# A graph network kernel on one core: sorting scatters issued in runs of five, each run answered by SP before the next

## What is computed

```python
edge_index = jnp.stack([src, dst])
h = jnp.maximum(_layernorm(x, axis=-1), 0.0)
x = x + _L0_gnn_ref(h, src, dst, ...)
h = jnp.maximum(_layernorm(x, axis=-1), 0.0)
x = x + _L1_gnn_ref(h, edge_index, ...)
h = jnp.maximum(_layernorm(x, axis=-1), 0.0)
x = x + _L2_gnn_ref(h, edge_attr_64, ..., edge_index, 3125)
h = jnp.maximum(_layernorm(x, axis=-1), 0.0)
x = x + _L3_gnn_ref(h, ..., src, dst)
```

## Time and profile before

| | us |
|---|---|
| median of 3 runs | 3888.61 |
| lowest and highest run | 3878.62, 3900.84 |
| the profiled execution, its own time | 3879.7 |
| span of its trace, first to last instruction | 3878.0 |
| share of the span: PE, DVE, ACT, POOL | 48%, 57%, 29%, 41% |
| granted TensorE clock, mean over the span | 0.663 of full speed |

### The profile page before, as it was taken

The page is one execution under the profiler, slowest core; times in us unless marked ns, Lnnn a source line. Parts: engine busy times, 40 slices in busy tenths (PEclk is TensorE's granted clock), DMA queues, the critical chain, the costliest instruction groups (busy, mean ns, idle before and its releaser), DMA issues. The chain is left out here.

```text
span 3878.0 us, 58297 instructions
## 1 busy us (share of the span) xinstructions
PE 1844.2 (48%) x16222; PEld 1335.8 (34%) x16222; DVE 2228.1 (57%) x4872; ACT 1128.6 (29%) x3658; POOL 1594.2 (41%) x1665
## 2 busy tenths in 40 slices
PE   6745555555545555411412147762111465665387
PEld 5623333333333333310101135751101355554222
DVE  7777777777777777411301013341111599997899
ACT  1154554445445454300001002100000011115644
POOL 1055555555555555376766640027676200000000
PEclk9865555555555555655655569975555689986599
DMA  7812221212112222622222210024443222220000
GB/s 250 307 41 43 46 43 43 43 43 46 42 43 43 43 44 47 246 65 51 60 54 53 51 34 1 12 82 125 121 115 76 74 87 78 88 78 31 0 0 9
DMA packets 399308, 267.12 MB, mean 69 GB/s; under 512 B 321456, under 2 KB 349293, under 8 KB 399073
## 3 DMA queue, kind: packets, MB, share of 16 engines
q1 hardware_dynamic: 306278, 87.81, 10.6%
q10 hardware_dynamic: 41472, 118.96, 8.4%
q0 software_dynamic: 51488, 59.40, 6.1%
HBM read 158.59 MB, written 107.47 MB: 69 GB/s over the span
## 5 line engine op out<-in xcount | busy, mean ns | idle before, releaser
L1241 POOL DMA_INDIRECT sorted_edges<-r_load,r_to x800 | 794.1, 993 | 675.0 <-DMA r_to<-places 364.6
L807 POOL DMA_INDIRECT hsrc<-h,edges x808 | 778.1, 963 | 593.1 <-PE ps L1004 361.4
L1004 PE MATMUL ps<-AO,hsrc 125*64 125x64 f32 x1616 | 195.9, 316 | 310.3 <-remote 252.7
L1555 ACT ACTIVATE w_work<-w_work 128x384 f32<-128x384 f32 (+1 forms) x160 | 85.8, 536 | 839.7 <-DVE w_work L1756 723.8
L1049 PE MATMUL ps<-hot,lo 125*128 125x400 bf16 (+2 forms) x1000 | 273.6, 456 | 100.9 <-DVE hot L866 70.8
L875 DVE TENSOR_TENSOR prod<-ps,hsrc 125x1024 f32<-125x1024 f32 x200 | 244.1, 1221 | 110.3 <-issue 107.8
L1004 PEld LDWEIGHTS ps<-AO,hsrc 125*64 125x64 f32 x1616 | 179.9, 224 | 346.0 <-issue 346.0
L1031 PE MATMUL ps<-rwin,there 120*125 120x256 bf16 x800 | 178.7, 397 | 242.4 <-DVE there L850 218.3
L866 DVE TENSOR_SCALAR hot<-ramp,small 125x400 bf16<-125x400 int16 x800 | 210.8, 321 | 143.5 <-issue 139.6
L1756 DVE TENSOR_TENSOR w_work<-ps,w_work 128x384 f32<-128x384 f32 (+1 forms) x160 | 90.9, 568 | 312.6 <-remote 264.9
L1409 PE MATMUL ps<-R 128*128 128x64 bf16 x3000 | 140.8, 208 | 247.0 <-DVE R L1745 121.9
(11 more groups left out here) (412 smaller groups left out, 3945.1 us busy)
## 6 DMA issues: line engine op xcount, KB each, us to landing
w_work<-sorted_edges ACTq DMA_DIRECT2D x42, 1000.0 KB
r_load<-in_edge_attr_dram SPq DMA_DIRECT2D x80, 312.5 KB
dstrow<-dst_rows SPq DMA_DIRECT2D x101, 234.4 KB
sorted_edges<-A ACTq DMA_DIRECT2D x10, 2000.0 KB, 9.8
A<-counts SPq DMA_DIRECT2D x12, 1600.0 KB
counts<-A ACTq DMA_DIRECT2D x4, 4000.0 KB, 31.7
sorted_edges<-A ACTq DMA_DIRECT2D x15, 1000.0 KB, 9.5
hsrc<-h,edges POOLq DMA_INDIRECT x808
```

What stands on the lines that cost most here:

```text
L807: g.indirect_dma_start(out=hsrc[:, s, t, :], out_offset=None, in_=S.h0[:, :], in_offset=bass.IndirectOffsetOnAxis(ap=edges.bitcast(I32)[:, ...
L1004: mm = pe.matmul(sums.rearrange("d (h w) -> d h w", h=H)[:, :, OFF[t]:OFF[t] + SUB], hsrc[0:TP, s, t, :], AO[0:TP, t, :, :], start=(t == 0 ...
L1241: g.indirect_dma_start(out=S.sorted, out_offset=bass.IndirectOffsetOnAxis(ap=to[:, hf, t:t + 1], axis=0), in_=load[:, hf, t, :], in_offset ...
```

## The change

HALF stays 10, RUN is 5, so that a chunk has RUNS = 4 runs. After each five scatters POOL adds one to `run` and waits for `go`. SP waits for `run`, adds three to `step` one by one (nobody waits for `step`), and then one to `go`. In `both(c)` the two answers of a half come before the wait for its landing. The semaphores that only carry waits are now one (`qr["carrier"]`).

```diff
+    STRIDE = 3
+    RUN = HALF // 2
+    RUNS = 2 * HALF // RUN
...
+            def follow(c, hf):
+
+                for r in range(RUNS // 2):
+                    sp.wait_ge(qr["run"], c * RUNS + hf * (RUNS // 2) + r + 1)
+                    for _ in range(STRIDE):
+                        sp.sem_inc(qr["step"], 1)
+                    sp.sem_inc(qr["go"], 1)
+
             def both(c):
 
                 for hf in range(2):
+                    follow(c, hf)
                     sp.wait_ge(qr[f"sc{hf}"], c * (16 * HALF) + 16 * HALF)
                     sp.sem_inc(qr["ready"], 1)
                     bring_half(nc, I, S, sp, c + 1, hf)
...
             for hf in range(2):
+                follow(C2 - 1, hf)
                 sp.wait_ge(qr[f"sc{hf}"], C2 * 16 * HALF)
...
                     for t in range(HALF):
                         g.indirect_dma_start(out=S.sorted, out_offset=bass.IndirectOffsetOnAxis(ap=to[:, hf, t:t + 1], axis=0),
                                              in_=load[:, hf, t, :], in_offset=None).then_inc(qr[f"sc{hf}"], 16)
+                        if t % RUN == RUN - 1:
+                            g.sem_inc(qr["run"], 1)
+                            g.wait_ge(qr["go"], c * RUNS + hf * (RUNS // 2) + t // RUN + 1)
+                            g.sem_inc(qr["carrier"], 1)
```

More of the change, by code:

```diff
@@ L1145, in spread @@
     props = [{n: sem(f"c_{n}{k}") for n in ("prod", "free", "own", "sum") if (n, k) != ("sum", 1)} for k in range(4)]
-    cl = {n: sem("k_" + n) for n in ("tp", "xt", "y", "t", "y1", "yfree", "hi", "r", "mid", "lo", "out", "wd", "carrier")}
-    qr = {n: sem("r_" + n) for n in ("sc0", "sc1", "ready", "carrier", "acarrier")}
+    cl = {n: sem("k_" + n) for n in ("tp", "xt", "y", "t", "y1", "yfree", "hi", "r", "mid", "lo", "out", "wd")}
+    qr = {n: sem("r_" + n) for n in ("sc0", "sc1", "ready", "carrier", "run", "step", "go")}
     qm = {n: sem("m_" + n) for n in (
@@ L1326, in turn_block @@
                 pe.wait_ge(cl["xt"], b + NB)
-                pe.sem_inc(cl["carrier"], 1)
+                pe.sem_inc(qr["carrier"], 1)
                 pe.transpose(S.bank[5][0:D, 0:P], fresh[:, m, :], S.ident[:, :]).then_inc(cl["tp"], 1)
@@ L1564, in _ @@
                 act.wait_ge(qm[f"es{s}"], n * 16 + 16)
-            act.sem_inc(qr["acarrier"], 1)
+            act.sem_inc(qr["carrier"], 1)
         @block.vector
```

## The result

| | before | changed |
|---|---|---|
| median, same chip (us) | 3883.61, 4 runs | 3526.94, 4 runs |
| lowest and highest | 3877.05, 3900.84 | 3497.86, 3531.55 |
| the profiled execution | 3879.7 | 3531.55 |
| its span | 3878.0 | 3529.8 |

The ratio is 0.907 (95% interval 0.904 to 0.910): 357 us less, where 190 were forecast. The time lies inside the range and on the side that was given 0.67. It lies 172 us under the forecast (3699) and 116 above the rival in which SP's signals carry PE's along (3411).

What follows compares the result with a forecast made beforehand. Signals held while scatters fly were taken to bound 1640 to 3046 us. With 9.3 us runs and the chain at 0.55, the last item ends at 3320 instead of 3510, giving 3690, plus 9 for the median: 3699 us, range 3440 to 3980.

Steps and rivals of the forecast that it cites:

- the rival in which SP's signals carry PE's along: Beside scatters, SP's increments let PE's held signals through: chain at 0.7, run 7.7 us, total 3411 us; chance 0.15.
- What bounded the kernel: From 1640 to 3046 us, scatters in flight hold PE's signals and slow SP's steps; POOL's pauses let them go.
- A run takes 9.3 us: In the sort, five scatters take 6.4 us plus a 2.9 us draining pause; between 6.75 and 13.1 us.
- SP's loads "just covered": SP's loads, 6.2 us a half, are as long as POOL's five scatters, so they should not delay answers.
- I take 0.55 for both stretches: Beside scatters, convolution and items go at 0.55 of free speed, with 0.4 and 0.8 as ends.
- The sum: After 1640 us: convolution done 2488, items from 2523, scatters until 3111, last item 3320 instead of 3510; gain 190 us.
- its likeliest case alone: Forecast for the whole kernel without rivals: 3560 to 3840 us, chance 0.46, nearly all of it faster.
- The moved scatters: 15 of chunk 23's scatters wait behind the convolution, costing POOL 19 us, which the compute chain gets as undisturbed time.
- The slower one: SP's answer is held like PE's signals: pause 6.1 us, run 12.5, total 3994 us, tipping at run 11.8; chance 0.24.
- The rival of prompt answers: Answers to POOL come in 0.35 us, scatters stay in flight, the chain creeps as before: 3883 us; chance 0.12.
- VectorE barring GpSimd: DVE work slows late scatters, five taking 9.3 us longer in 67 runs: about 4138 us in all; chance 0.03.
- The signs that were named: In the changed profile: gaps 2 to 4 us behind each five, last scatter near 3110, convolution wait under 60 us.

Runs made afterwards that it cites:

- its nearest relative: Changed kernel with SP answering each run with one increment instead of four; on chips without held signals, ratios 1.081, 1.076 and 1.078 against the kernel before.

## Why the prediction was right, and where its sizes were off

**What bounded the kernel: right for this chip.** Held signals were read from a few stalls and from the busy shares. The changed kernel shows signals arriving in the pauses, and the two kernels that differ by POOL's wait alone, 3564 and 3863 us, show that its waiting is what pays. What is held was read too narrowly: not only PE's signals but the steps of PE and SP themselves, 0.70 us and multiples of it. And "pauses of POOL let them go" left out that the pauses of the kernel before, 60 us of them until 2290, did it late or not at all. The chips on which no signal is held show the same from the other side: DVE works beside the scatters there without any pause. That a chip of the second kind exists could not be seen in the one trace of before.

**"A run takes 9.3 us": the step that failed.** It rested on "I take 2.9", a pause behind every five in which the scatters drain. Measured: nothing behind the second five of a half, and 3.3 on the mean behind the first. The answer does not wait for a drain at all, nor even for the writing: POOL's signal goes 4.4 or 8.0 us before the fifth scatter is written. POOL reached the wait for the convolution at 2330.6 instead of 2468, so the 90 runs from 1637.0 took 694 us, 7.7 each. The other 67, from 2361.0 to 2939.6, took 8.6.

**SP's loads "just covered": wrong, and the reason for the pause.** The sum of 6.2 us was about right (6.06 at 1913.67). It left out when the loads begin: 1.7 us after the half's last scatter is written. So they end 1.4 us after POOL's next five, and POOL's next scatter starts another 1.2 us later. Had I laid the start of the loads beside POOL's five, this would have stood in the sum. SP starts them soon now: 1.7 us after the half's last scatter, where the median of the kernel before is 5.4.

**"I take 0.55 for both stretches": too low.** By the prediction's own working, 475 us of work are due until the convolution ends. The last 29 ran in POOL's wait, so 446 fell in the 691 us before: 0.65. For the items 23 of 13.3 us in 540 us give 0.57, though POOL paused less than assumed. The term that was too small is the free time after a pause: 2 us of it from `attend`, with 1.4 of the pause itself, 3.4 in a run of 9.3, while the trace has some 7 us in each half of 15.2. With the prediction's own 0.3 for the rest that gives, as an estimate, 0.46 + 0.54 x 0.3 = 0.62.

**The sum.** With 7.7 and 8.6 us for a run and 0.65 and 0.57 for the chain: POOL's wait at 2331, the convolution done at 2360, items from about 2400 (forecast 2523), last scatter 2939 (3111), 160 - 93 = 67 adds or 17 items of 13.3 left, end at 3163 (3320; the last add L1773 starts at 3158). The 157 us between the forecast and this are nearly the whole error: 3699 - 3527 = 172. Both sizes were wrong in the same direction, and the gain is nearly twice the one forecast. The time lies outside what the prediction gave its likeliest case alone (3560 to 3840); that it lies in the range is owed to the width left for the rival at 3411, whose reason was not the right one.

**The moved scatters** cost and gave what was said: POOL waited 30.5 us before 2361, and the chain's last 29 us ran undisturbed.

**The rivals.** The slower one, an answer that is held as PE's signals are, did not come. Pauses of six microseconds are not the rule: the mean is 3.3, and a mean run of 7.7 or 8.6 us is far from the tip of 11.8. Behind 2361, of the eight pauses over 5 us five follow loads of 8.4 to 10.8 us, which the chips without held signals show too, and the others loads that begin 3.8 to 5.0 us after the half instead of 1.7. The rival of prompt answers was half right. After the second five of a half the answer is prompt, so prompt that POOL does not stop; if it had been so after each, the nearest run is the kernel without the wait, which gained 31 us. The rival of SP's signals that carry PE's along fits the times best (7.7 us a run, POOL's wait at 2325, 0.7), but for another reason: its runs are short because every second answer is free. Its own effect, read without POOL's wait, is those 31 us at most; whether the increments do more together with a pause was not run where signals are held. VectorE barring GpSimd: a scatter beside the items takes 333.71 / 315 = 1.06 us, against 1.004, and 1.09 in the kernel without the wait on a chip without held signals (366.27 / 336, stretch 2000 to 2473), where DVE is busy 350 of 473 us. By the Trainium skill's rule (SBUF — State Buffer, SBUF: two separate sides), that descriptors and VectorE's two-port modes exclude each other, the trace agrees in sign; it is some 0.06 us a scatter, 18 us in all, where 1.86 a scatter was priced for the rival.

**The signs that were named.** Convolution wait under 60 us: 23. More than 20 items before the last scatter: 23. PE's share over 35%: 59%. Right. Last scatter near 3110 and gaps behind each five: wrong, as above. The sign that was named for SP's increments, gaps under 1 us with DVE busy, is met by every second gap; the kernel without the wait decides that it did not mean them.

**What stays open.** Whether a pause without SP brings the same where signals are held (the kernels for it met only chips without); whether four increments are better than one there, or pauses after every five; whether it matters that POOL is silent while SP issues the last of its loads, as it is in these pauses; what in the chip slows the steps of PE and SP and lets a held signal go, and why one kind of chip holds them and the other does not. No version beat the rest on both kinds: the changed kernel is the best of the three run where signals are held, and the kernel before, or the one without POOL's wait, the best of those run on the three other chips.

## What to carry to other kernels

When every engine is idle beside a stream of indirect DMAs, look how late each signal arrives after its producer's end. Look also how far apart an engine's instructions are that wait for nothing. If it is microseconds, a short, regular stop of the issuing engine can pay: about 240 us of pauses bought 299 us here, since the engine had to wait for the others later anyway. Where such a stop is made of a handshake, look when the signal is really given, since the queue can run ahead of the work, and what the answering engine is doing at that moment, since that sets the length of the stop, far more than the number of increments does. And run both kernels on more than one chip before keeping such a change: it is 9% faster on one kind, while its nearest relative is 8% slower on the other.

## What the runs showed that I had not expected

- The same program takes 3884 and 3894 us in two of the comparisons and 2873 to 2878 in three, each on another chip. In `attend` alone POOL's waits for PE are 362 us on the one kind and 128 on the other.
- POOL's signal behind five indirect DMAs goes 4.4 to 8.0 us (medians) before the fifth is written, so a prompt answer leaves the gap of 0.30 us as it is.
- Where signals are held, PE's products that wait for nothing start 0.7 to 3.5 us apart beside the scatters; on the three other chips never more than 0.2.
- A wait for five scatters to land takes 2.7 to 3.7 us, and a fill with a wait for its own signal about half a microsecond (three make a gap of 1.75).
